# First expert product of a mixture in three passes of rounded halves instead of one full-precision product

## What is computed

```python
xn = (x - mu) * rsqrt(var + EPS) * ln_gamma + ln_beta
abel_out = gelu(xn @ abel_w + abel_b)
logits = xn @ moe_gate_w + moe_gate_b
topw, topi = top_k(logits, 2)                      # softmax over the two
h  = gelu(einsum('bsd,edh->ebsh', xn, ew1) + eb1)  # 8 experts, 128 -> 256
eo = einsum('ebsh,ehd->ebsd', h, ew2) + eb2        # 256 -> 128
moe_out = einsum('ebsd,bse->bsd', eo, w_dense)     # then three rotations
gate = sigmoid(concat([abel_out, moe_out]) @ gc_w + gc_b)
mixed = abel_out * (1 - gate) + moe_out * gate     # + residual
```

## Time and profile before

| | |
|---|---|
| time, median of 3 runs | 1156.88 us (1151.92, 1157.06, 1156.88) |
| profiled execution | 1151.51 us, of which its span 1150.2 us |
| PE busy | 1088.7 us (95%) |
| DVE busy | 934.0 us (81%) |
| ACT busy | 700.5 us (61%) |
| POOL busy | 423.3 us (37%) |
| chain of work that ended last | PE 76%, DVE 14%, ACT 5% |
| DMA | 15.33 MB, nearly all in the first 30 us and 100 to 200 us |

### The profile page before, as it was taken

One profiled execution on the slowest core, in us unless ns is written; L12 is line 12 of the kernel. 1 busy time (PEld: TensorE's weight loads), 2 busy tenths in 40 slices (PEclk: granted clock), 3 DMA queues, 4 the chain that ended last, 5 costly groups with the idle time before them and its releaser, 6 DMA issues.

```text
span 1150.2 us, 23195 instructions
## 1 busy us (share of the span) xinstructions
PE 1088.7 (95%) x7617; PEld 791.4 (69%) x7617; DVE 934.0 (81%) x3323; ACT 700.5 (61%) x1806; POOL 423.3 (37%) x707
## 2 busy tenths in 40 slices
PE   6789699999989999999999999999999999999997
PEld 5688466666666867677777777777777777656776
DVE  3986989899988698788888888888888888656767
ACT  1255356555656567777776767676767777645441
POOL 4410223332224155444444444444444555431310
PEclk9999999999999999999999999999999999999999
DMA  9200300000000000000000000000000000000000
GB/s 280 58 2 1 111 1 2 1 1 2 1 1 1 1 1 2 1 2 1 1 2 1 2 1 1 2 1 2 1 2 1 1 2 2 1 1 8 9 8 16
DMA packets 19957, 15.33 MB, mean 13 GB/s; under 512 B 2432, under 2 KB 18816, under 8 KB 19712
## 3 DMA queue, kind: packets, MB, share of 16 engines
q1 hardware_dynamic: 19840, 13.86, 4.2%
HBM read 12.81 MB, written 1.05 MB: 12 GB/s over the span
## 4 chain that ended last, share of the span: by engine, by line
PE 76%; DVE 14%; ACT 5%; issue 3%; POOL 1%; DMA 0%; SPq 0%; DVEq 0%; ACTq 0%; POOLq 0%
PE bank L1669 12%; PE bank L1699 11%; PE bank L1663 10%; PE bank L1618 8%; PE bank L2007 5%; PE bank L1047 5%; PE bank L2028 4%; PE bank L1639 3%; PE bank L1647 3%; PE bank L1032 2%; ACT prb L1734 2%; PE bank L648 2%; DVE prob L1418 2%; PE bank L1025 1%; DVE moe L2202 1%
## 5 line engine op out<-in xcount | busy, mean ns | idle before, releaser
L1765 POOL TENSOR_SCALAR prb<-prb,rnorm 128x512 f32<-128x512 f32 (+3 forms) x512 | 271.8, 549 | 348.1 <-DVE rnorm L1855 348.0
L1734 ACT ACTIVATE prb<-prb,negmax 128x512 f32<-128x512 f32 (+3 forms) x512 | 280.9, 552 | 113.3 <-DVE negmax L1837 113.3
L1837 DVE CUSTOM_DVE_ANT_0 prb<-bank,mask 128x512 f32<-128x512 f32 (+3 forms) x512 | 218.7, 483 | 18.4 <-PE bank L1663 18.4
L1669 PE MATMUL bank<-ident,prb 128*128 128x128 f32 x1280 | 158.3, 275 | 3.4 <-POOL prb L1765 2.9
L1669 PEld LDWEIGHTS bank<-ident,prb 128*128 128x128 f32 x1280 | 139.6, 141 | 23.0 <-issue 12.0
L1699 PE MATMUL bank<-prbT,vv 128*64 128x512 f32 (+3 forms) x1024 | 151.9, 439 | 0.0
L1699 PEld LDWEIGHTS bank<-prbT,vv 128*64 128x64 f32 x1024 | 63.4, 136 | 82.1 <-issue 81.9
L1742 ACT ACTIVATE prbT<-bank 128x512 f32<-128x512 f32 x128 | 76.5, 598 | 61.9 <-PE bank L1669 61.1
L1846 DVE COPY prbT<-bank 128x512 f32<-128x512 f32 x128 | 87.8, 690 | 14.8 <-PE bank L1669 14.4
L1734 ACT ACTIVATION_READ_ACCUMULATOR prb<-prb,negmax 128x1 f32 x512 | 96.8, 189 | 0.0
L2065 ACT ACTIVATE h<-bank,eb1T 128x512 f32<-128x512 f32 x64 | 43.7, 687 | 53.8 <-PE bank L2007 53.6
(11 more groups left out here) (472 smaller groups left out, 2370.8 us busy)
## 6 DMA issues: line engine op xcount, KB each, us to landing
x<-in_x SPq DMA_DIRECT2D x2, 512.0 KB, 6.1
ew2T<-in_ew2T SPq DMA_DIRECT2D x1, 1024.0 KB, 8.1
ew<-in_ew SPq DMA_DIRECT2D x1, 1024.0 KB, 5.5
wq<-in_Wq SPq DMA_DIRECT2D x2, 512.0 KB, 4.9
wk<-in_Wk SPq DMA_DIRECT2D x2, 512.0 KB, 7.1
wv<-in_Wv SPq DMA_DIRECT2D x1, 1024.0 KB, 8.0
out<-res SPq DMA_DIRECT2D x16, 64.0 KB, 1.5
wmod<-in_wmod SPq DMA_DIRECT2D x2, 384.0 KB, 6.9
```

The costliest lines, as they stand in the source:

```text
L1669: last = T.transpose(into[:, at + (qc - kc) * P:at + (qc - kc + 1) * P], prb[j % 2][:, i, p_at[qc] + kc * P:p_at[qc] + (kc + 1) * P], iden ...
L1734: A.activation(v, v, ACT.Exp, scale=-1.0, bias=negmax[j % 2][:, place[qc], i:i + 1], accum_out=rowsum[j % 2][:, place[qc], i:i + 1]).then_ ...
L1765: last = G.tensor_scalar(v, v, rnorm[j % 2][:, place[qc], i:i + 1], 1.0, ALU.mult, ALU.mult)
L1837: V.tensor_tensor_reduce(prb[j % 2][:, i, p_at[qc]:p_at[qc] + (qc + 1) * P], s_of(j, s, i, qc), mask[:, (NT - 1 - qc) * P:S], 1.0, LARGEST ...
```

## The change

`widen` becomes three passes of float32r halves, as the attention's projections already are: high weights x high tokens, low weights x high tokens, high weights x low tokens, into the same bank. For that:

- The weights are split once, in the attention's last batch. In `late(j)` of steps 53 to 56 ACT copies a quarter of ew1 (128x512) into `ew1_hi`, and POOL subtracts it into `ew1_lo`. They lie where the attention's first projection weights and `h3[0]` were.
- The tokens are split per batch in a new step `halves(b)`: ACT copies `hTm` into `hT_hi`, DVE subtracts into `hT_lo` (both over `hT1`, which is dead by then). halves(0) comes in step 63 before the logits, halves(1) in step 64 before `lean(0)`, halves(2) and halves(3) at the end of the mixture's batches 0 and 1, after the last close.
- Some tiles are placed elsewhere (`scrap`, `res` and `abel` of the last batch), and DVE's `turn(b)` for b >= 2 waits for the abel product of b-2 too, since the tokens are read from `hTm` by that product and by the logits only.

```diff
+        SPLIT_EW1 = PER * (B - 1) + 5
...
             def late(j):      # attention_scalar
+                n = j - SPLIT_EW1
+                if 0 <= n < 4:
+                    if n == 0:
+                        A.wait_ge(at_proj, 2 * (PER * (B - 1) + 4))
+                        A.wait_ge(at_vps, PER * (B - 1) + 4)
+                    A.activation(ew1_hi[:, 2 * n:2 * n + 2, :], ew1[:, 2 * n:2 * n + 2, :], ACT.Copy).then_inc(at_whi, 1)
...
             def late(j):      # attention_gpsimd
+                n = j - SPLIT_EW1
+                if 0 <= n < 4:
+                    G.wait_ge(at_whi, 4 + n + 1)
+                    part = slice(2 * n, 2 * n + 2)
+                    G.tensor_tensor(ew1_lo[:, part, :], ew1[:, part, :], ew1_hi[:, part, :].bitcast(F32), ALU.subtract).then_inc(at_w, 1)
...
                 if place == 2:
+                    halves(0)
                     logits(0)
...
             if j == UNITS:
                 if place == 0:
+                    halves(1)
                     lean(0)
...
                 squash(b, NT - 1)
                 close(b, NT - 1)
+                if after:
+                    halves(after)
                 if b + 1 < B:
                     bias(b + 1)
...
-                    T.wait_ge(mx_h, 1)
                     T.wait_ge(*((at_pta, 2 * UNITS), (at_ptv, 3 * UNITS))[j])
-                T.matmul(F01[j % 2][:, :], ew1[:, j // HC, (j % HC) * P:(j % HC + 1) * P], hTm[b % 2], start=True, stop=True).then_inc(mx_up, 1)
+                if b == 0 and j == 0:
+                    T.wait_ge(at_w, len(w3) + 4)
+                if j == 0:
+                    T.wait_ge(mx_hhi, b + 1)
+                    T.wait_ge(mx_hlo, b + 1)
+                for k, (w, h) in enumerate(((ew1_hi, hT_hi), (ew1_lo, hT_hi), (ew1_hi, hT_lo))):
+                    last = T.matmul(F01[j % 2][:, :], w[:, j // HC, (j % HC) * P:(j % HC + 1) * P], h[b % 2], start=(k == 0), stop=(k == 2))
+                last.then_inc(mx_up, 1)
...
+            def halves(b):    # mixture_scalar
+                A.wait_ge(mx_h, b + 1)
+                if b >= 2:
+                    A.wait_ge(mx_up, HALF * (b - 1))
+                else:
+                    A.wait_ge(at_h, B)
+                A.activation(hT_hi[b % 2], hTm[b % 2], ACT.Copy).then_inc(mx_hhi, 1)
...
+            def halves(b):    # mixture_vector
+                V.wait_ge(mx_hhi, b + 1)
+                V.tensor_tensor(hT_lo[b % 2], hTm[b % 2], hT_hi[b % 2].bitcast(F32), ALU.subtract).then_inc(mx_hlo, 1)
```

## The result

The changed kernel is a little faster. Its median is 1147.06 us (6 runs), that of the kernel before 1152.23 (6 runs, three of them those that the prediction started from); the ratio is 0.996, 95% interval 0.9944 to 0.9976. The profiled executions have spans of 1150.2 (before) and 1145.5 us (after). The median of the kernel before that the prediction started from, 1156.88, was on the upper of two levels in which its executions fall; with more runs the median went to the lower one. Forecast was a saving of 7.1 us, measured are 4.7 between the profiles, 5.2 between the medians, and 5.3 in the profiles from the first product with ew1 to the end.

The account below looks back on a forecast made before the run. TensorE was taken as the bound until about 1132 us, then DVE. Groups of four 6.0 + batch 0 2.0 - waits 0.86 = 7.1 us saved, from 1156.9 to about 1149.5 us; range 1142.5 to 1153.5.

Parts of the forecast that it names:

- the price of three passes: Mixture's products with ew1: three passes take 0.69 us against 0.905; by TensorE's time alone 64 products save 13.8 us.
- the limit of two banks: Mixture's products: product n needs ACT to have read product n-2, so a group of four saves 0.50 us, not 0.86.
- The group of four: Four products with ew1 between contracts: from 3.62 to 3.12 us; 12 groups in batches 1 to 3 save 6.0 us.
- where TensorE comes too early: Batch 1: TensorE waits for batch 2's expert weights and ACT's normalising of batch 3; takes back 0.86 us.
- the splits cost nothing: Splitting ew1 in attention steps 53 to 56: cost 0, or up to 2.0 us if the cover is gone.
- the port, for the new operations: New DVE and POOL subtractions: DVE can be held by POOL on the shared port; cost 0 to 0.5 us, taken as 0.
- "saves 0.4" behind the detour: Products from 1027.57 to 1032.05 us, around the turning of batch 1's expert weights: 4.48 becomes 4.1 us.
- the three signs: Wrong if: passes over 0.24 us apart, clock below 1.00 before 1120 us, or POOL releasing the turning in steps 53 to 57.
- its slower rival: Mixture: more idle TensorE lowers its clock; mean 0.90 would add 12 us, slower by 5, 1162 us; chance 0.04.
- six products in a row: Batch 0's run of six products with ew1: from 5.76 to 4.86 us, saves 0.9.
- the 5.8 to 9: Whole kernel: the saving in us that counts as the forecast case; chance 0.56.
- given back: Batch edges: token halves on ACT and DVE delay TensorE three times, 3.2 us saved remain, 1153.7 us; chance 0.25.

Follow-up runs that it names:

- e2: Changed kernel without the middle pass (low weights x high tokens), so two passes a product; one execution, 1142.72 us.
- e4: Changed kernel with products in pairs, two between the halves of each contract and two behind, with some groups kept at four; 1144.78 us, ratio 0.9926 to the kernel before.
- e1: Changed kernel with all splitting kept but one float32 product again, the halves unused; ratio 1.0000 to the kernel before.
- e8: Changed kernel with nine more float32r passes, results unused, put where TensorE stands 2.25 us; 1146.14 us, ratio 0.9946 to the kernel before.
- e3: Changed kernel with four products of batch 0 moved ahead of ACT's lean(1) behind the attention's end; 1143.50 us, ratio 0.9924 to the kernel before.
- The three orders alone: Kernel before, float32 product, with pairs, products ahead of lean(1) and earlier expert weights; 1148.36 us, ratio 0.9970 to the kernel before.
- e0: Changed kernel run again, unaltered; 1146.34 us, ratio 0.9951 to the kernel before.
- e6: Changed kernel with the next batch's expert weights and DVE's shift moved to the end of tile 1; 1145.25 us, ratio 0.9941 to the kernel before.

## Why the prediction was right or wrong

**Right: the price of three passes and the limit of two banks.** The group of four was laid out at 3.12 us and measures 3.15; e2 and e4 show that it is the hole of ACT's Gelu and not TensorE's rate. That it fits so closely is partly luck, since two offsets cancel: in the first products the Gelu starts 1.00 us after the first pass (1009.81 to 1010.81) and not 0.89, and the third product's matmul starts together with its weight load, at 1011.55, and not 0.11 later. The page "FP8 and Floating Point Precision" of the Trainium skill (section "TensorE Precision Notes") gives four passes for true FP32, hence, as an estimate by that page, a quarter less for three. The rows come near to it: 0.70 against 0.905 us a product where nothing waits (1.40 a pair in e4), 23% less. A group gets a bit over half of that.

**Right: where TensorE comes too early.** In batch 1 the changed kernel has both waits, 0.25 us for the expert weights (laid out at 0.4) and 0.51 us behind ACT's normalising (laid out at 0.45; in brackets: idle before, and for whom):

```profile
1088.00 0.60 PE L2026 MATMUL bank<-ident,wde 128*8 128x128 f32 x4 [0.25 <-DVE wde L2223]
...
1090.51 0.51 PE L2041 MATMUL bank<-hT_hi,ew_hi 128*128 128x512 f32 x1 [0.51 <-ACT h L2108]
```

Batch 1 saved 1.06 us where 1.14 was forecast. From 1074.36 to the product at 1090.51 its chain runs over DVE and ACT, and two operations of DVE lie on it that run beside POOL's residual and take far longer than elsewhere:

```profile
1077.45 1.25 DVE L2260 CUSTOM_DVE_ANT_0 scrap<-moe,gc_w 128x128 f32<-128x128 f32 x1
...
1079.01 1.18 DVE L2269 SCALAR_TENSOR_TENSOR res<-moe,gate,res 128x128 f32<-128x128 f32 x1
```

Elsewhere they take 0.29 and 0.35 us. The kernel before has the same two (1.19 and 1.18), off its chain. So by the trace 1.8 us of DVE's chain in batch 1 come from working beside POOL, more than the two waits together; no run moves POOL's residual to test it.

**Right: the splits cost nothing.** In attention step 53 ACT's copy takes 0.62 and pushes its two PSUM copies back, and POOL's subtraction takes 1.29 and uses up the 1.31 us of the earlier trace rows (the order of time on ACT, then on POOL):

```profile
913.27 0.62 ACT L1771 ACTIVATE ew_hi<-ew 128x512 fp32r<-128x512 f32 x1
913.79 1.07 ACT L1756 ACTIVATE prbT<-bank 128x512 f32<-128x512 f32 x2
```

```profile
916.07 1.29 POOL L1794 TENSOR_TENSOR ew_lo<-ew,ew_hi 128x512 fp32r<-128x512 f32 x1
917.34 2.89 POOL L1785 TENSOR_SCALAR prb<-prb,rnorm 128x512 f32<-128x512 f32 x5
```

POOL has no idle time left between the two normalisings, and the turning of steps 53 to 57 keeps its distance to the kernel before (0.66 or 0.67 us later at each, the start's loss). e1 confirms it for all the splits.

**Nearly nothing: the port, for the new operations.** The new subtraction of halves(0) on DVE took 1.00 us instead of 0.69, beside POOL's normalising, which ends at 1005.97:

```profile
1005.50 1.00 DVE L2186 TENSOR_TENSOR hT_lo<-hTm,hT_hi 128x512 fp32r<-128x512 f32 x1
```

This is what the page "SBUF — State Buffer" of the Trainium skill (section "SBUF: two separate sides") says of a DVE operation with two SBUF inputs beside a GpSimd one, that it waits until the other has ended; the trace agrees, with 0.31 us more. It lay under TensorE's abel product and cost nothing, within the bound that was given.

**Wrong: "saves 0.4" behind the detour.** The step took the matmuls of 1027 to 1032 at the full clock. In the changed kernel that stretch cost 0.94 us more than before; in e8, with the clock held, it saved 0.34, near the 0.4 of the forecast. Two of the three signs that the prediction named for being wrong came true there: passes over 0.24 us apart, and a clock below 1.00 before 1120 us. The prediction did have TensorE's clock as its slower rival, but at the wrong place and size: it thought of the small holes in each group, over the whole mixture, for 12 us. In the groups the clock stayed at 1.00 throughout, and it fell at one standstill, for 3.5 us and 1.3 us of loss. That this standstill was harmless before was taken as if it would remain so.

**A little off: six products in a row.** Laid out at 4.86 us, measured 5.14. The third and the fifth product start at 1.74 and 3.49, as laid out; the last pair takes 1.65 us and not 1.38. Of that 0.11 is the first pass behind a hole, which takes 0.34 us to the next and not 0.23: its load starts with it (both 1013.30), and the second pass's load only at 1013.41. The rest is the step to the next kind of product.

**The chances.** I gave 0.73 to faster by over 0.5%. The measured 0.4 to 0.5% lies at that edge, on the side of no change. The chance was too high because 7.1 us stood only 1.3 above the bound, and a single term of 1.3 us, the low clock at one place, was enough. As a saving, the 5.2 us lie below the 5.8 to 9 to which I gave 0.56, and above the 3.2 of "given back". The time that I named, 1149.5, is 2.4 above the measured 1147.06. It lies that near partly by luck: the starting median was 4.7 too high and the saving was put 1.9 too high, and the two errors pull in opposite directions.

## What to carry to other kernels

Before a product is made cheaper, lay out one group with its consumer: with two PSUM banks the third product waits for the first one's reader, and here 0.35 us a group was lost to that (tiles of 6.72 against 6.37 us) until other matmuls were put between the pairs. When a change makes TensorE's work shorter, look at each place where it already stood still, because the clock can fall there though it did not before; moving ready work in front of the instruction that waits took away both the standstill and the low clock here (e3). The three orders alone gave 4.0 us, the cheaper product alone 5.2, and both together 11.5 (1152.4 to 1140.9).

## What the runs showed of the hardware that I had not expected

A standstill of TensorE of 2.25 us was followed by some 3.5 us at a granted clock of 0.50 in the changed kernel, in e0 and, at the same place of the program, in e6; in e4, after 2.24 us, by 3.2 us. With 1.93 us of standstill among float32 products (the kernel before) it was not. With two passes (e2, 2.14 us) the low level lasted from 1027.4 past 1037 us, though TensorE was busy all that time.
